# A spectral filter block: the gated spectrum is laid out channel by channel, and the inverse column transform becomes one 128-column and two 64-column matmuls a channel

## The chip, the cores and the metric

The program runs on one core of a Trainium2 chip. The metric is the device time of one execution in microseconds (us); lower is better. Three runs of the kernel before gave 4968.33, 4972.34 and 4972.80 us, median 4972.34 us.

## What is computed

The reference has two layers in a row. The change touches the first one, on x of shape (4 images, 128 rows, 128 columns, 128 channels), all in fp32:

```
f    = fft2(x) over rows and columns, per image and channel
amp  = |f|
gate = sigmoid(amp @ w_h + b_h) + sigmoid(amp @ w_l + b_l)      # a matmul over channels at each frequency
s    = real(ifft2(f * gate))
y    = layernorm(swish(conv3x3(s, w_f) + b_f) + x) * gamma + beta
```

The second layer is a Mamba-like sequence block (projections, a short convolution, a scan over 256 steps in chunks, gating, a feed-forward part). It is not changed, but rows of it are used below.

## The kernel before, in words

The first layer is `spectral_block`. Each engine has a program of its own; they are kept in step by semaphores alone, and each engine runs its instructions in the order written. One image is done after the other (loop `b`, 4 passes). Because x is real, only 65 of the 128 row frequencies are kept; real and imaginary part of the 64 full ones fill 128 rows, and the two edge frequencies (0 and 64), which have one real row each after the first transform, share the slots of row 0.

The stages of an image, with the lines by which the profile names them:

1. **Row transform.** 128 matmuls (L235) of the image's columns against a DFT table. ScalarE (L332) and VectorE (L444) take turns to copy the results from PSUM into `rowspec` [128, 128 frequencies, 128 channels]. The copy goes through PSUM in order and writes each next element 128 words (512 bytes) further on.
2. **Column transform.** Matmuls L250 to L253 by cosine and sine tables; ScalarE and VectorE store the real part, the imaginary part and the amplitude in `spec` [128, 3 x 64, 128 channels]. Before the change its three blocks of 64 rows stand in the order amplitude, real, imaginary.
3. **Gating.** 17 groups (16 of four frequencies, one for the edges) run through a pipeline: TensorE turns the amplitudes (L274), VectorE copies them (L473), TensorE multiplies by the two gate weights (L286), ScalarE takes two sigmoids (L356), VectorE adds them (L480), TensorE turns the sum back (L295), and VectorE multiplies real and imaginary rows by it in place (two instructions of L489 a group; `gate` is read from PSUM). The edges are finished at L496 and L499. In VectorE's program step q does the copy of group q, then the add of group q-1, then the two multiplications of group q-2. GpSimd follows behind each group and writes the negated imaginary rows over the amplitude rows that are no longer needed (L528), so that `spec` holds (-imaginary, real, imaginary).
4. **Inverse column transform.** For each of the 128 channels two matmuls of 128 stationary columns and 128 moving columns accumulate in one PSUM region: L306 has (real, imaginary) of the channel as the stationary operand and the cosine table as the moving one, L307 has (-imaginary, real) and the sine table. The stationary operand of a channel is 128 words that stand 512 bytes apart in `spec`. Both wait for `gated` and for GpSimd's `neg_done`. Every four channels fill one of four PSUM banks; ScalarE (L361) and VectorE (L503) take turns to copy a bank into `rowspec`, now [128, column, channel].
5. **Inverse row transform and 3x3 convolution.** L194 reads `rowspec` column by column, L370 and L398 split the result into two halves in a ring (`s_hi`, `s_lo`), and 27 matmuls for each block of four columns (L211 to L213) make the convolution. Swish, residual and layernorm follow, behind TensorE, and SyncE loads the residual (`xres`) and stores the result. `s_hi`, `s_lo` and the other buffers of this stage lie over `spec`.

In the second layer there are matmuls with 32 stationary columns. `mix` first does two matmuls with 128 stationary columns (L931) and then eight with 32 (L935), one for each head, whose outputs lie on different 32-partition quarters of PSUM:

```
for h in range(HEADS):
    j, low = h // 4, HEADDIM * (h % 4)
    mm = pe.matmul(ps[low:low + HEADDIM, bank, at + j * P:at + (j + 1) * P], dtx[...], mmat[...], ...)
```

An fp32 matmul of the program shows in the trace as two LDWEIGHTS and two MATMUL records, one after the other; so L306 and L307, with 512 matmuls each, have 1024 records each. "Record" below is such a half.

Of the kernel before, what the change touches and what calls it, by code (L numbers as in the profile page):

```python
# [18 lines left out]
ALU = mybir.AluOpType  # L19
ACT = mybir.ActivationFunctionType  # L20

P = 128
IMAGES, H, W, C = 4, 128, 128, 128
# [4 lines left out]
HALF = H // 2  # L28
# [27 lines left out]
def spectral_block(nc, a, z1):  # L56
    ctx = ExitStack()
    counted = []
    with ctx:
# [4 lines left out]
        def sems(name, n):  # L64
# [5 lines left out]

        spec = sb("spec", [P, 3 * HALF, C])

        rowspec = sb("rowspec", [P, P, C])
# [14 lines left out]

        over = Place(nc, "f_", spec_at)
        s_hi = over("s_hi", [P, RING + 2, H + 2], FR)  # L90
        s_lo = over("s_lo", [P, RING + 2, H + 2], FR)
        conv_v = over("conv_v", [P, 2, 512])
        xres = over("xres", [P, 2, 512])
# [13 lines left out]
            sem("f_" + n) for n in ("edge_mm", "edge_copied", "edge_sq", "edge_ss", "edge_amp_ready"))  # L107
        ampT_mm, ampT_ready, gate_mm, sig_ready, gsum_ready, gT_mm, gated, neg_done, edge_scaled = (
            sem("f_" + n) for n in ("ampT_mm", "ampT_ready", "gate_mm", "sig_ready", "gsum_ready",
                                    "gT_mm", "gated", "neg_done", "edge_scaled"))  # L110
        t_mm, t_free = sem("f_t_mm"), sems("f_t_free", 4)
# [76 lines left out]
        def _(pe):  # L188
            def columns(b, j):

                if j >= 4:
                    pe.wait_ge(lo_ready, b * BLOCKS + (j - 3))
                for k in range(4):
                    mm = pe.matmul(ps[:, j % 4, k * P:(k + 1) * P], rowspec[:, 4 * j + k, :], idft_h[:, :],  # L194
                                   start=True, stop=True)
                mm.then_inc(s_mm, 1)
# [31 lines left out]
            with pe.Fori(0, IMAGES) as b:  # L228
# [37 lines left out]
                for q in range(G17 + 2):  # L266
                    if q < G17:
                        if q >= 2:
                            pe.wait_ge(ampT_ready, b * G17 + (q - 1))
                        if q == GROUPS:  # L270
                            pe.wait_ge(edge_amp_ready, b + 1)
                        for k in range(4 if q < GROUPS else 2):
                            src = spec[:, 4 * q + k, :] if q < GROUPS else edge_amp[:, k, :]
                            mm = pe.transpose(ps[:, q % 2, k * P:(k + 1) * P], src, ident[:, :])  # L274
                        mm.then_inc(ampT_mm, 1)
# [23 lines left out]
                pe.wait_ge(gated, b * G17 + G17)  # L299
                pe.wait_ge(neg_done, b * G17 + G17)  # L300
                for j in range(C // 4):
                    if j >= 4:
                        pe.wait_ge(t_free[j % 4], b * 8 + j // 4)
                    for k in range(4):
                        out = ps[:, j % 4, k * P:(k + 1) * P]
                        pe.matmul(out, spec[:, HALF:3 * HALF, 4 * j + k], cosm[:, :], start=True, stop=False)  # L306
                        mm = pe.matmul(out, spec[:, 0:2 * HALF, 4 * j + k], sinm[:, :], start=False, stop=True)  # L307
                    mm.then_inc(t_mm, 1)
# [13 lines left out]
        def _(act):  # L322
# [5 lines left out]
            with act.Fori(0, IMAGES) as b:  # L328
# [6 lines left out]
                with act.Fori(0, GROUPS // 2) as q:  # L335
                    for s in range(2):
                        act.wait_ge(f_mm[s], b * 8 + q + 1)
                        act.activation(spec[:, ds(q * 8 + s * 4 + HALF, 4), :],
                                       ps[:, 2 * s, :].rearrange("p (r c) -> p r c", r=4), ACT.Copy)
                        act.activation(work[:, 2 * s, :], ps[:, 2 * s, :], ACT.Square).then_inc(re_ready[s], 1)  # L340
                        act.wait_ge(ss_ready[s], b * 8 + q + 1)
                        act.activation(spec[:, ds(q * 8 + s * 4, 4), :],
                                       work[:, 4 + s, :].rearrange("p (r c) -> p r c", r=4),
                                       ACT.Sqrt).then_inc(amp_ready[s], 1)
# [14 lines left out]
                for j in range(0, C // 4, 2):  # L359
                    act.wait_ge(t_mm, b * 32 + (j + 1))  # L360
                    act.activation(rowspec[:, :, 4 * j:4 * j + 4],  # L361
                                   ps[:, j % 4, :].rearrange("p (c w) -> p w c", c=4), ACT.Copy).then_inc(t_free[j % 4], 1)
# [23 lines left out]
        def _(dve):  # L386
# [53 lines left out]
            with dve.Fori(0, IMAGES) as b:  # L440
# [8 lines left out]
                with dve.Fori(0, GROUPS // 2) as q:  # L449
                    for s in range(2):  # L450
                        dve.wait_ge(f_mm[s], b * 8 + q + 1)
                        im = spec[:, ds(q * 8 + s * 4 + 2 * HALF, 4), :]
                        dve.tensor_copy(im, ps[:, 2 * s + 1, :].rearrange("p (r c) -> p r c", r=4)).then_inc(im_ready[s], 1)
# [13 lines left out]
                for q in range(G17 + 2):  # L467
# [14 lines left out]
                    if q >= 2:  # L482
                        g = q - 2
                        dve.wait_ge(gT_mm, b * G17 + (g + 1))
                        gate = ps[:, 6 + g % 2, :].rearrange("p (r c) -> p r c", r=4)
                        if g < GROUPS:
                            for row in (HALF + 4 * g, 2 * HALF + 4 * g):
                                part = spec[:, row:row + 4, :]
                                ins = dve.tensor_tensor(part, part, gate, ALU.mult)  # L489
                            ins.then_inc(gated, 1)  # L490
                        else:


                            for k in range(2):
                                part = edge[:, 2 * k:2 * k + 2, :]
                                ins = dve.tensor_tensor(part, part, gate[:, k:k + 1, :].to_broadcast([P, 2, C]), ALU.mult)  # L496
                            ins.then_inc(edge_scaled, 1)
                            dve.wait_ge(edge_scaled, b + 1)
                            dve.tensor_tensor(spec[:, HALF:3 * HALF:HALF, :], edge[:, 0:2, :], edge[:, 2:4, :],  # L499
                                              ALU.add).then_inc(gated, 1)  # L500
                for j in range(1, C // 4, 2):
                    dve.wait_ge(t_mm, b * 32 + (j + 1))
                    dve.tensor_copy(rowspec[:, :, 4 * j:4 * j + 4],  # L503
                                    ps[:, j % 4, :].rearrange("p (c w) -> p w c", c=4)).then_inc(t_free[j % 4], 1)
# [895 lines left out]
```

## Time and profile before

| | |
|---|---|
| median of three runs | 4972.34 us |
| profiled execution | 4973.1 us, span 4971.3 us |
| TensorE matmul busy | 4777.4 us (96%) |
| VectorE busy | 3626.1 us (73%) |
| ScalarE busy | 3136.8 us (63%) |
| GpSimd busy | 1884.9 us (38%) |
| mean granted TensorE clock | 0.983 of full speed |

The span runs from the first to the last instruction of the program; the execution adds 1.8 us around it. A row of the timeline gives the start, the length, engine, line and tiles of a run of like instructions and their count; the length of a merged row is from the first start to the last end. PE is a matmul, PEld a weight load, which may lie beside matmuls. The records of TensorE overlap, since a matmul's record goes on after the next has begun; a busy TensorE is therefore not one at its peak, and the distance of two starts tells more than a duration. PEclk is the granted clock in tenths or as a share of full speed.

### The profile page before, as it was taken

What the parts mean: (1) busy time and instruction counts of PE and PEld (TensorE: products, weight loads), DVE (VectorE), ACT (ScalarE), POOL (GpSimd) and SP (SyncE); (2) the same over time, 40 slices, a digit from 0 to 9 for tenths busy, and PEclk for the clock granted to TensorE, in tenths of its full rate; (3) what the DMA queues carried; (4) which work ended last, traced back from release to release, by engine and by line L of the source; (5) the groups of instructions that cost most, each with busy time, mean ns of one, the idle gap of its engine ahead of it and who ended that gap; (6) DMA issues with size and microseconds to landing.
All of it is one profiled execution on the core that took longest, in us unless ns stands there. A gap on an engine that the chain in (4) does not pass through costs nothing.

```text
span 4971.3 us, 93964 instructions
## 1 busy us (share of the span) xinstructions
PE 4777.4 (96%) x31687; PEld 3555.1 (72%) x31687; DVE 3626.1 (73%) x9341; ACT 3136.8 (63%) x4388; POOL 1884.9 (38%) x2150
## 2 busy tenths in 40 slices
PE   7999999999999999969999999999999999999998
PEld 4888669875988498736766666666667666666766
DVE  4346542655166615659999999999999999999997
ACT  4211421133112411159999999999999999999997
POOL 0011000110011001135566556656655665566564
PEclk9999999999999999979999999999999999999999
DMA  2012201230023001211111111111111111111110
GB/s 78 1 50 70 85 1 35 70 100 0 20 70 99 17 5 62 68 38 37 36 36 36 36 38 36 36 36 36 36 36 38 36 36 36 36 38 36 36 36 24
DMA packets 216359, 205.38 MB, mean 41 GB/s; under 512 B 15904, under 2 KB 150688, under 8 KB 216224
## 3 DMA queue, kind: packets, MB, share of 16 engines
q1 hardware_dynamic: 216224, 203.58, 13.1%
q8 instruction: 85, 1.39, 0.1%
q14 instruction: 50, 0.41, 0.0%
HBM read 136.41 MB, written 67.11 MB: 41 GB/s over the span
## 4 chain that ended last, share of the span: by engine, by line
PE 30%; ACT 23%; issue 3%; DVE 0%; ACTq 0%; POOL 0%; POOLq 0%; DVEq 0%
PE g_ps L935 6%; PE g_ps L931 5%; PE g_ps L874 4%; ACT g_acc L1041 3%; ACT L1101 3%; ACT L1135 3%; PE g_ps L919 3%; ACT g_tap L1046 3%; PE g_ps L903 3%; ACT g_emat L1078 2%; PE g_ps L920 2%; PE g_ps L965 2%; ACT L1098 2%; ACT g_gl L1093 2%; ACT g_bmat L1054 2%
## 5 line engine op out<-in xcount | busy, mean ns | idle before, releaser
L1186 DVE SCALAR_TENSOR_TENSOR g_acc<-g_ps,g_conv_w,g_acc 128x504 f32<-128x504 f32 (+2 forms) x896 | 651.6, 727 | 11.6 <-ACT g_tap L1046 11.6
L1243 DVE TENSOR_TENSOR g_mmat<-g_emat,g_ps 128x1024 f32<-128x1024 f32 x512 | 616.5, 1204 | 1.5 <-PE g_ps L892 0.8
L381 ACT ACTIVATE f_conv_v<-f_ps,f_bias 128x512 f32<-128x512 f32 x128 | 87.9, 687 | 782.3 <-PE f_ps L213 782.3
L1078 ACT ACTIVATE g_emat<-g_ps 128x1024 f32<-128x1024 f32 x512 | 494.4, 1017 | 44.3 <-PE g_ps L920 44.3
L919 PE MATMUL g_ps<-g_rz,g_l 128*128 128x512 f32 x1024 | 481.6, 532 | 27.7 <-ACT g_emat L1078 25.1
L211 PE MATMUL f_ps<-f_s_hi,f_wf_hi 128*128 128x512 f32 x1152 | 468.4, 407 | 2.3 <-DVE f_s_lo L398 2.3
L213 PE MATMUL f_ps<-f_s_hi,f_wf_lo 128*128 128x512 f32 x1152 | 457.9, 397 | 0.0
L212 PE MATMUL f_ps<-f_s_lo,f_wf_hi 128*128 128x512 f32 x1152 | 457.1, 397 | 0.0
L768 POOL TENSOR_TENSOR g_sqs<-g_sq 128x256 f32<-128x256 f32 x256 | 186.7, 729 | 660.6 <-ACT g_sq L1083 660.6
L920 PE MATMUL g_ps<-g_mask_b,g_ident_b 128*128 128x512 bf16 x1024 | 400.2, 391 | 0.0
L540 POOL TENSOR_SCALAR f_rstd<-f_mv 128x4 f32<-128x4 f32 x128 | 40.9, 320 | 839.4 <-DVE f_mv L414 839.4
L503 DVE COPY f_rowspec<-f_ps 128x512 f32<-128x512 f32 x64 | 44.2, 691 | 412.2 <-PE f_ps L307 412.2
L931 PEld LDWEIGHTS g_ps<-g_xs,g_diag 128*128 128x128 f32 x2048 | 277.7, 190 | 88.5 <-issue 88.3
L935 PE MATMUL g_ps<-g_mmat,g_dtx 128*32 128x128 f32 x8192 | 329.8, 279 | 0.0
L773 POOL TENSOR_TENSOR g_acc<-g_acc,g_tap 128x508 f32<-128x508 f32 x256 | 326.1, 1274 | 4.3 <-DVE g_acc L1186 4.3
L931 PE MATMUL g_ps<-g_xs,g_diag 128*128 128x128 f32 x2048 | 326.0, 282 | 1.2 <-ACT g_emat L1078 1.2
L306 PE MATMUL f_ps<-f_cosm,f_spec 128*128 128x128 f32 x1024 | 309.7, 385 | 9.8 <-POOL f_spec L528 9.8
L1284 DVE TENSOR_SCALAR g_hn<-g_z,g_mv,g_r 128x128 f32<-128x128 f32 x512 | 315.9, 676 | 1.7 <-POOL g_r L791 1.7
L307 PE MATMUL f_ps<-f_sinm,f_spec 128*128 128x128 f32 x1024 | 309.3, 384 | 0.0
L361 ACT ACTIVATE f_rowspec<-f_ps 128x512 f32<-128x512 f32 x64 | 38.2, 597 | 417.6 <-PE f_ps L307 417.6
L1041 ACT ACTIVATE g_acc<-g_ps,g_conv_b,g_conv_w 128x512 f32<-128x512 f32 x384 | 283.0, 772 | 6.2 <-PE g_ps L862 6.2
L306 PEld LDWEIGHTS f_ps<-f_cosm,f_spec 128*128 128x128 f32 x1024 | 272.5, 313 | 10.7 <-DVE f_spec L499 10.7
(178 smaller groups left out, 12118.7 us busy)
## 6 DMA issues: line engine op xcount, KB each, us to landing
f_xt<-in_x_cols SPq DMA_DIRECT2D x128, 256.0 KB, 2.9
f_xres<-in_x SPq DMA_DIRECT2D x128, 256.0 KB, 2.7
z<-f_zout SPq DMA_DIRECT2D x128, 256.0 KB, 2.1
g_zin<-z SPq DMA_DIRECT2D x128, 256.0 KB, 2.7
g_zres<-z SPq DMA_DIRECT2D x128, 256.0 KB, 2.7
out<-g_outb SPq DMA_DIRECT2D x128, 256.0 KB, 2.0
f_wf_raw<-in_w_f SPq DMA_DIRECT2D x1, 576.0 KB, 5.1
g_wx<-in_in_proj_t SPq DMA_DIRECT2D x1, 192.0 KB, 2.5
```

The lines of the kernel that those rows point to most:

```text
L211: pe.matmul(out, wf_hi[:, tap, :], hi, start=(tap == 0), stop=False)
L212: pe.matmul(out, wf_hi[:, tap, :], lo, start=False, stop=False)
L213: mm = pe.matmul(out, wf_lo[:, tap, :], hi, start=False, stop=(tap == 8))
L306: pe.matmul(out, spec[:, HALF:3 * HALF, 4 * j + k], cosm[:, :], start=True, stop=False)
L919: pe.matmul(dst, l4[:, g, :], rz[:, 4 * half:4 * half + 4, :], start=True, stop=False)
L920: mm = pe.matmul(dst, ident_b[:, :], mask_b[:, :].unsqueeze(1).to_broadcast([P, 4, P]), start=False, stop=True)
L931: pe.matmul(ps[:, bank, at + j * P:at + (j + 1) * P], diag[:, j, :], xs[:, x.s, j, g, :], start=(g % 2 == 0 and j == 0), stop=False)
L935: mm = pe.matmul(ps[low:low + HEADDIM, bank, at + j * P:at + (j + 1) * P], dtx[:, g // 2, at + HEADDIM * h:at + HEADDIM * (h + 1)], mmat[: ...
L1041: act.activation(acc[:, j], four(ps[:, X_BANK[j] if j < 2 else BC_BANK, :]), ACT.Identity, bias=conv_b[:, j:j + 1], scale=conv_w[:, j, 3:4 ...
L1078: act.activation(emat[:, g, :].rearrange("p (b n) -> p b n", b=2), ps[:, D_BANK[g]:D_BANK[g] + 2, :], ACT.Exp).then_inc(e_a[g], 1)
L1186: dve.scalar_tensor_tensor(out=acc[:, j, :, k:], in0=four(ps[:, bank, :])[:, :, 0:P - k], scalar=conv_w[:, j, 3 - k:4 - k], in1=acc[:, j, ...
L1243: dve.tensor_tensor(mmat[:, g, :].rearrange("p (h n) -> p h n", h=HEADS), emat[:, g, :].rearrange("p (h n) -> p h n", h=HEADS), ps[:, CB, ...
```

## The change

Spectrum: `spec` now has its blocks in the order real, imaginary, amplitude (the indices at stage 2 and in the transposes of stage 3 follow). The gated spectrum is no longer written in place. L489 writes into a new tensor `gains` [128, channel, 128 rows], so that the 128 words of a channel stand side by side; the multiplication's output walks 512 bytes from one element to the next, its inputs are read as before. L499 writes its two rows there too. GpSimd's negation and the semaphore `neg_done` are gone.

Inverse column transform: three matmuls a channel in place of two. The first has all 128 columns of `gains[:, c, :]` as the stationary operand and the cosine table. The second has the 64 imaginary columns and the negated sine table, and writes PSUM partitions 0 to 63. The third has the 64 real columns and the sine table, and writes partitions 64 to 127. Both accumulate onto the first.

Places: `gains` takes the place of `rowspec`; the result of the inverse column transform is a tensor `inv` that takes the place of the real and imaginary rows of `spec`; `s_hi` and `s_lo` lie over `gains`, the other buffers of stage 5 over the amplitude rows. The copies L361 and L503 have the same shapes and strides as before.

```diff
-                pe.wait_ge(neg_done, b * G17 + G17)
                 for j in range(C // 4):
                     if j >= 4:
                         pe.wait_ge(t_free[j % 4], b * 8 + j // 4)
                     for k in range(4):
-                        out = ps[:, j % 4, k * P:(k + 1) * P]
-                        pe.matmul(out, spec[:, HALF:3 * HALF, 4 * j + k], cosm[:, :], start=True, stop=False)
-                        mm = pe.matmul(out, spec[:, 0:2 * HALF, 4 * j + k], sinm[:, :], start=False, stop=True)
+                        at, c = slice(k * P, (k + 1) * P), 4 * j + k
+                        pe.matmul(ps[:, j % 4, at], gains[:, c, :], cosm[:, :], start=True, stop=False)
+                        pe.matmul(ps[0:HALF, j % 4, at], gains[:, c, HALF:], nsinm[:, :], start=False, stop=True)
+                        mm = pe.matmul(ps[HALF:P, j % 4, at], gains[:, c, 0:HALF], sinm[:, :], start=False, stop=True)
                     mm.then_inc(t_mm, 1)
...
-                            for row in (HALF + 4 * g, 2 * HALF + 4 * g):
-                                part = spec[:, row:row + 4, :]
-                                ins = dve.tensor_tensor(part, part, gate, ALU.mult)
+                            for k in range(2):
+                                ins = dve.tensor_tensor(gains[:, :, HALF * k + 4 * g:HALF * k + 4 * g + 4].rearrange("p c r -> p r c"),
+                                                        spec[:, HALF * k + 4 * g:HALF * k + 4 * g + 4, :], gate, ALU.mult)
                             ins.then_inc(gated, 1)
...
-                            dve.tensor_tensor(spec[:, HALF:3 * HALF:HALF, :], edge[:, 0:2, :], edge[:, 2:4, :],
+                            dve.tensor_tensor(gains[:, :, 0:2 * HALF:HALF].rearrange("p c k -> p k c"), edge[:, 0:2, :], edge[:, 2:4, :],
                                               ALU.add).then_inc(gated, 1)
...
-                for g in range(G17):
-                    pool.wait_ge(gated, b * G17 + (g + 1))
-                    pool.sem_inc(waited)
-                    first, last = (max(4 * g, 1), 4 * g + 4) if g < GROUPS else (0, 1)
-                    pool.tensor_scalar(spec[:, first:last, :], spec[:, 2 * HALF + first:2 * HALF + last, :], -1.0, 1.0,
-                                       ALU.mult, ALU.mult).then_inc(neg_done, 1)
```

## Rows read from the trace of the kernel before

**Rows 1.** The page, busy time of each engine (share of the span), instructions

```profile
PE 4777.4 (96%) x31687; PEld 3555.1 (72%) x31687; DVE 3626.1 (73%) x9341; ACT 3136.8 (63%) x4388; POOL 1884.9 (38%) x2150
```

**Rows 2.** Busy time by stretch: gating, inverse column transform, convolution of image 1

```profile
core 0: us, PE busy (x) PEld busy (x) DVE busy (x) ACT busy (x) POOL busy (x), PEclk, DMA share, GB/s
116.00:171.90 55.90, 48.70 (x200) 28.38 (x200) 42.70 (x71) 23.14 (x37) 10.10 (x17) 0.93 0.00 1
171.90:285.50 113.60, 112.76 (x512) 112.60 (x512) 11.06 (x16) 9.55 (x16) 0.62 (x4) 0.98 0.00 1
285.50:532.00 246.50, 245.80 (x1244) 204.78 (x1244) 147.35 (x548) 43.14 (x71) 41.02 (x63) 1.00 0.23 71
```

**Rows 3.** Waits from 172 to 285 us: total, times, longest (us)

```profile
ACT f_rowspec L361 <- PE f_ps L307: 104.5, 16, 8.1
```

**Rows 4.** Timeline, TensorE in the inverse column transform: start, length, count

```profile
178.17 0.60 PE L306 MATMUL f_ps<-f_cosm,f_spec 128*128 128x128 f32 x2
178.61 0.60 PE L307 MATMUL f_ps<-f_sinm,f_spec 128*128 128x128 f32 x2
179.05 0.60 PE L306 MATMUL f_ps<-f_cosm,f_spec 128*128 128x128 f32 x2
```

**Rows 5.** Groups by line, weight loads: busy us, mean ns, idle before

```profile
L306 PEld LDWEIGHTS f_ps<-f_cosm,f_spec 128*128 128x128 f32 x1024 | 272.5, 313 | 10.7 <-DVE f_spec L499 10.7
L194 PEld LDWEIGHTS f_ps<-f_idft_h,f_rowspec 128*128 128x128 f32 x1024 | 135.6, 195 | 14.8 <-issue 4.2
```

**Rows 6.** Timeline, 128-column and 32-column matmuls in turn (second layer), then their loads

```profile
2514.06 0.61 PE L931 MATMUL g_ps<-g_xs,g_diag 128*128 128x128 f32 x4
2514.60 0.65 PE L935 MATMUL g_ps<-g_mmat,g_dtx 128*32 128x128 f32 x16
2515.17 0.71 PE L931 MATMUL g_ps<-g_xs,g_diag 128*128 128x128 f32 x4
2515.81 0.64 PE L935 MATMUL g_ps<-g_mmat,g_dtx 128*32 128x128 f32 x16
...
2514.60 0.38 PEld L935 LDWEIGHTS g_ps<-g_mmat,g_dtx 128*32 128x32 f32 x16
2515.17 0.52 PEld L931 LDWEIGHTS g_ps<-g_xs,g_diag 128*128 128x128 f32 x4 [0.20 <-issue]
```

**Rows 7.** One line's durations (min/median/max ns), and a run of 128-column matmuls

```profile
L935 PE MATMUL g_ps<-g_mmat,g_dtx x8192: 272/273/298, 2190.2 to 4947.9; 128*32 128x128 f32 x200
...
2504.35 1.95 PE L953 MATMUL g_ps<-g_wc,g_ygt 128*128 128x128 f32 x16
```

**Rows 8.** Timeline, VectorE in the gating stage, one round of two groups

```profile
151.02 0.68 DVE L473 COPY f_work<-f_ps 128x512 f32<-128x512 f32 x1
153.61 0.68 DVE L473 COPY f_work<-f_ps 128x512 f32<-128x512 f32 x1
155.07 0.69 DVE L480 TENSOR_TENSOR f_work<-f_work 128x512 f32<-128x512 f32 x1 [0.78 <-ACT f_work L356]
155.68 1.28 DVE L489 TENSOR_TENSOR f_spec<-f_spec,f_ps 128x512 f32<-128x512 f32 x2
156.88 0.68 DVE L473 COPY f_work<-f_ps 128x512 f32<-128x512 f32 x1
```

**Rows 9.** Groups by line, VectorE: busy us, mean ns, idle before

```profile
L489 DVE TENSOR_TENSOR f_spec<-f_spec,f_ps 128x512 f32<-128x512 f32 x128 | 81.7, 680 | 0.0
L503 DVE COPY f_rowspec<-f_ps 128x512 f32<-128x512 f32 x64 | 44.2, 691 | 412.2 <-PE f_ps L307 412.2
L444 DVE COPY f_rowspec<-f_ps 128x512 f32 x64 | 65.8, 1036 | 85.2 <-PE f_ps L235 77.7 <-issue 7.5
```

**Rows 10.** Timeline, the last steps of the gating stage

```profile
170.91 0.42 DVE L499 TENSOR_TENSOR f_spec<-f_edge 128x256 f32<-128x256 f32 x1
171.52 0.30 POOL L528 TENSOR_SCALAR f_spec<-f_spec 128x128 f32<-128x128 f32 x1 [0.50 <-DVE f_spec L499]
171.97 0.78 PE L306 MATMUL f_ps<-f_cosm,f_spec 128*128 128x128 f32 x2 [2.46 <-POOL f_spec L528]
```

**Rows 11.** Busy time by stretch, the first 4.1 us of the transform (granted clock: 0.50)

```profile
172.00:176.10 4.10, 4.10 (x19) 4.10 (x20) 0.00 (x0) 0.24 (x1) 0.00 (x0) 0.50 0.00 0
```

More of the change, by code:

```diff
@@ L71, in spectral_block @@
         spec = sb("spec", [P, 3 * HALF, C])
+        row_at = sb.at
         rowspec = sb("rowspec", [P, P, C])
@@ L87, in spectral_block @@
         mhalf = sb("mhalf", [P, 4])
-        over = Place(nc, "f_", spec_at)
+        amp_at = row_at - HALF * C * 4
+        gains = Place(nc, "f_", row_at)("gains", [P, C, 2 * HALF])
+        inv = Place(nc, "f_", spec_at)("inv", [P, W, C])
+        over = Place(nc, "f_", row_at)
         s_hi = over("s_hi", [P, RING + 2, H + 2], FR)
         s_lo = over("s_lo", [P, RING + 2, H + 2], FR)
+        over = Place(nc, "f_", amp_at)
         conv_v = over("conv_v", [P, 2, 512])
@@ L107, in spectral_block @@
             sem("f_" + n) for n in ("edge_mm", "edge_copied", "edge_sq", "edge_ss", "edge_amp_ready"))
-        ampT_mm, ampT_ready, gate_mm, sig_ready, gsum_ready, gT_mm, gated, neg_done, edge_scaled = (
+        ampT_mm, ampT_ready, gate_mm, sig_ready, gsum_ready, gT_mm, gated, edge_scaled = (
             sem("f_" + n) for n in ("ampT_mm", "ampT_ready", "gate_mm", "sig_ready", "gsum_ready",
-                                    "gT_mm", "gated", "neg_done", "edge_scaled"))
+                                    "gT_mm", "gated", "edge_scaled"))
         t_mm, t_free = sem("f_t_mm"), sems("f_t_free", 4)
@@ L193, in columns @@
                 for k in range(4):
-                    mm = pe.matmul(ps[:, j % 4, k * P:(k + 1) * P], rowspec[:, 4 * j + k, :], idft_h[:, :],
+                    mm = pe.matmul(ps[:, j % 4, k * P:(k + 1) * P], inv[:, 4 * j + k, :], idft_h[:, :],
                                    start=True, stop=True)
@@ L272, in _ @@
                         for k in range(4 if q < GROUPS else 2):
-                            src = spec[:, 4 * q + k, :] if q < GROUPS else edge_amp[:, k, :]
+                            src = spec[:, 2 * HALF + 4 * q + k, :] if q < GROUPS else edge_amp[:, k, :]
                             mm = pe.transpose(ps[:, q % 2, k * P:(k + 1) * P], src, ident[:, :])
@@ L337, in _ @@
                         act.wait_ge(f_mm[s], b * 8 + q + 1)
-                        act.activation(spec[:, ds(q * 8 + s * 4 + HALF, 4), :],
+                        act.activation(spec[:, ds(q * 8 + s * 4, 4), :],
                                        ps[:, 2 * s, :].rearrange("p (r c) -> p r c", r=4), ACT.Copy)
@@ L341, in _ @@
                         act.wait_ge(ss_ready[s], b * 8 + q + 1)
-                        act.activation(spec[:, ds(q * 8 + s * 4, 4), :],
+                        act.activation(spec[:, ds(q * 8 + s * 4 + 2 * HALF, 4), :],
                                        work[:, 4 + s, :].rearrange("p (r c) -> p r c", r=4),
@@ L360, in _ @@
                     act.wait_ge(t_mm, b * 32 + (j + 1))
-                    act.activation(rowspec[:, :, 4 * j:4 * j + 4],
+                    act.activation(inv[:, :, 4 * j:4 * j + 4],
                                    ps[:, j % 4, :].rearrange("p (c w) -> p w c", c=4), ACT.Copy).then_inc(t_free[j % 4], 1)
@@ L451, in _ @@
                         dve.wait_ge(f_mm[s], b * 8 + q + 1)
-                        im = spec[:, ds(q * 8 + s * 4 + 2 * HALF, 4), :]
+                        im = spec[:, ds(q * 8 + s * 4 + HALF, 4), :]
                         dve.tensor_copy(im, ps[:, 2 * s + 1, :].rearrange("p (r c) -> p r c", r=4)).then_inc(im_ready[s], 1)
@@ L502, in _ @@
                     dve.wait_ge(t_mm, b * 32 + (j + 1))
-                    dve.tensor_copy(rowspec[:, :, 4 * j:4 * j + 4],
+                    dve.tensor_copy(inv[:, :, 4 * j:4 * j + 4],
                                     ps[:, j % 4, :].rearrange("p (c w) -> p w c", c=4)).then_inc(t_free[j % 4], 1)
```

## The prediction, written before the result was known

> **What bounds the kernel now.** I read the page's busy times first. TensorE is busy for 96% of the span and no other engine for more than 73% [rows 1], but that is an average over two layers, and the change touches two stages of one. So the next view is the busy time by stretch. In image 1 the gating stage takes 55.9 us and the inverse column transform 113.6 us; the other three images show the same lengths within 1 us. In the transform VectorE and ScalarE work for 11 and 10 us of it, and matmuls and weight loads both fill it [rows 2]. The waits of that stretch agree: ScalarE's copies wait 104.5 us for L307 [rows 3]. What TensorE needs for a channel is what the stage costs, with nothing behind it to take over: the four copies of 16 columns go on at 3.5 us a bank, and one takes 0.7 us.
>
> The timeline gives the price of a channel. L306 starts at 178.17, L307 at 178.61, the next L306 at 179.05: 0.44 us a matmul, 0.88 a channel, and 128 of them make 112.6 of the 113.6 us [rows 4]. That is 0.22 a record. Elsewhere TensorE is twice as fast with the same shape: 16 records of L953 in 1.95 us, the last of which takes 0.27, are 1.68 / 15 = 0.112 a record [rows 7]. The weight loads show why: one of L306, whose words stand 512 bytes apart, takes 313 ns, one of L194, whose words stand side by side, 195 [rows 5]. The transform is bound by strided weight loads.
>
> The gating stage has another bound. VectorE is busy for 42.7 of 55.9 us and TensorE for 48.7 [rows 2], but neither is full; it is a ring of dependences. The copy of a group starts at 151.02, and the add of the same group at 155.07, when its sigmoid is there: 4.05 us, in which another group's copy (153.61) is slipped in and VectorE idles for 0.78. From 155.07 to the copy at 156.88 are the add and two multiplications. So two groups take 4.05 + 1.81 = 5.86 us, and only every second group's multiplications lie on that ring [rows 8].
>
> **The transform after the change.** All its weight loads become contiguous, so a record costs 0.112 and not 0.22. Two matmuls of 128 columns would then take 0.45 us a channel. But there are three matmuls, and TensorE has to change between 128-column and 64-column form twice a channel, 1024 times in all. The second layer shows what such a change costs, with 32 columns for 64 [rows 6]. The last record of L931 starts at 2514.06 + 0.61 - 0.27 = 2514.40, and the first load of L935 only at 2514.60, 0.20 later, where a load otherwise lies beside the matmul before it. The last record of L935 starts at 2514.98, and the next load of L931 at 2515.17, again 0.20 later, after an idle time of 0.20 that the row itself shows; its first product then has to wait for that load too. The whole turn of 4 records with 128 columns and 16 with 32 takes 2515.81 - 2514.60 = 1.21 us. The 16 lie beside each other: their starts span 0.65 - 0.27 = 0.38 us, which is four rounds of four (three steps of 0.112, 0.025 for the first load, since the longest of its records takes 298 ns and the median 273 [rows 7], 0.02 of issue). So each quarter of the columns has its own queue, and neighbours in program order that use one quarter don't hold up the others.
>
> A channel has 2 records with 128 columns and 4 with 64, on two halves: two rounds. Against the 1.21 us that is two full records less (0.224), two rounds less (0.224), and a first load of 64 columns in place of 32 (0.025 more): 1.21 - 0.224 - 0.224 + 0.025 = 0.79 us. It saves 0.88 - 0.79 = 0.09 us a channel, for 512 channels 46 us. Bounds: with no cost of the changes of form, four rounds, 0.45 us (220 us saved); with the four records of the sine part one after the other, 0.79 + 0.22 = 1.01 us (67 us lost). I take 0.79, since rows 6 are the nearest thing to the new loop.
>
> The Trainium skill has a rule that would put the price higher. TensorE: Matmul & The Clock Gate, "The mechanism" in its part on packing small matmuls, says that matmuls are strictly first in, first out in start and end. Each sine matmul is two records on one half of the columns, so by that rule the order would be first half, then both halves at once, then second half: three rounds for two. Rows 6 speak against it: in the same order the 16 records of L935 would need nine rounds, and their starts would span 8 x 0.112 = 0.9 us where they span 0.38.
>
> **The clock.** At the start of the transform the granted clock is 0.50 for 4.1 us, and costs nothing today, since the weight loads set the pace [rows 11]: 19 records in 4.1 us are 0.22 each, as later [rows 4]. The matmuls on TensorE just before are sparse (the last groups of the gating), and that stays. After the change a round takes 0.21 us at 1.2 GHz and not 0.11, a channel 0.79 + 4 x 0.107 = 1.22. In 4.1 us 3.4 channels are done and not 5.2: 1.4 us an image, 6 in all. Bounds 0 and, if the slow stretch were twice as long, 12.
>
> **The gating after the change.** L489 now walks 512 bytes from one written element to the next. L444 writes in just this way, from PSUM, with the same shape: 1036 ns, where L503, which writes 16 bytes at a stride, takes 691 and L489 today 680 [rows 9]. So a multiplication grows by 0.355 us. Bounds: 0.01 (as L503) and 0.5. On the ring of rows 8 one group's two multiplications lie, so two groups take 5.86 + 0.71 = 6.57 us; VectorE's own work for two groups (four multiplications at a distance of 0.95, two copies and two adds at 0.60) is 6.2, still below. Seven times 0.71, and the last two groups, behind which nothing waits any more, with 0.71 each: 6.4 us an image. If instead every group's growth counted, 16 x 0.71 = 11.4.
>
> The end of the stage gets shorter. L499 starts at 170.91, GpSimd's last negation at 171.52, the first matmul at 171.97 [rows 10]. The negation's 0.30 and the hop to it go, 0.6 us less; L499 writes 256 elements at the stride and grows by half of 0.355, 0.2 more. The other 16 negations were behind VectorE and cost nothing. Sum of the gating: 6.4 - 0.6 + 0.2 = 6.0 us an image, 24 us in all; from -2 to +44 by the bounds.
>
> **At no cost.** The copies L361 and L503 keep their shape, and a bank comes every 3.2 us and not 3.5. The order of `spec` changes places and no strides. `wf_raw`, `xres` and `zout` lie elsewhere; SyncE's loads start on the same counts, and the next image's first copies write over `s_hi` and `s_lo` only behind matmuls that TensorE issues after its last convolution, so they wait for nothing new. L194 reads `inv` as it read `rowspec`. With the gating slower, ScalarE and TensorE idle more in it; both have room.
>
> **The sum.** -46 + 6 + 24 = -16 us against the profiled execution's 4973.1 us, 4957.1; that execution was 0.8 us above the median of the three runs, so 4956 us. Only 0.03 us a channel lies between this and no gain: it breaks even at 0.82 us.
>
> **Rivals.**
> - The sine matmuls take three rounds, because their two records on one half follow each other. The place is the transform, the price 0.112 x 512 = 57 us: 5013 us, slower. It decides as soon as a channel costs over 0.82 us. For it speaks that no row has 64-column matmuls, against it rows 6. With four rounds, 5070.
> - The strided multiplication costs nothing, as L503's stride does: -46 + 6 - 2 = -42, 4930 us. Against it, L444 has the same stride and L503 has not.
> - VectorE becomes the bound in the gating: the ring breaks up and each group pays 0.71. 16 x 0.71 - 0.4 = 11 us an image, 44 in all: +4, 4976 us, no change. For it speaks that 6.57 and 6.2 are close.
> - The changes of form cost less with 64 columns, as low as the step of 0.112 between rounds. A channel takes some 0.6 us, 143 us saved: about 4860 us. Against it, both directions show 0.20.
> - The clock stays at 1.2 GHz through the transform, since TensorE now pauses 1024 times. A channel takes 1.22: (1.22 - 0.88) x 512 + 24 = 198, 5170 us. Against it, the turns of rows 6 run at full speed, in a stage with denser work around them.
>
> **How the numbers follow.** The forecast has 0.50, with a range of its own of 4940 to 4975. Three rounds 0.15, four 0.04, a free stride 0.10, VectorE as the bound 0.12, cheap changes of form 0.05, the slow clock 0.04. A measurement of this kernel can tell 0.2% (10 us) from no change. Below 4962 lie some 0.36 of the forecast's 0.50, the free stride and the cheap changes: 0.51 faster. The rest of the forecast and VectorE's case, 0.26, are no change. Three and four rounds and the clock, 0.23, are slower. The range goes from 4915 to 5015 us: it holds the forecast, the free stride, VectorE's case and three rounds, and leaves out 0.13 and a little of the edges.
>
> **What would show it.** In the trace after, the distance of two cosine matmuls should be 0.79 us (0.60, 0.90 or 1.22 for the rivals), the weight loads of 128 columns some 190 ns and not 313, and an idle time of 0.20 before each of them. The transform should take 102 to 103 us an image and not 113.6, the gating 62 and not 55.9. L489 should take 1.04 us, with two groups every 6.6 us. The prediction is wrong if a channel costs over 0.82 us or under 0.75, or if the gating grows by over 10 us or not at all.

## The result: 263 us slower, and the transform ran at half clock

The changed kernel takes 5233.08 us (median of 4 runs, 5231.5 to 5236.5) against 4970.35 us for the kernel before in the same comparison: a ratio of 1.0529, 95% interval 1.0511 to 1.0548. The forecast was 4956 us, in a range of 4915 to 5015, so the sign and the size are both wrong. The span of the profiled execution is 5234.7 us and the mean granted clock 0.918 where it was 0.983.

The page after, busy time of each engine and the line of the granted clock in 40 slices (9 is 90% or more of full speed):

```profile
PE 5030.0 (96%) x32711; PEld 3521.4 (67%) x32711; DVE 3660.9 (70%) x9341; ACT 3136.0 (60%) x4388; POOL 1840.7 (35%) x2082
PEclk9669995899669995897999999999999999999999
```

TensorE is 96% busy as before [rows 1]; the busy share says nothing of the loss. The clock line does: it dips once in each of the four images (the single 7 behind them stands in the line of the kernel before too). The same three stretches of image 1 as in [rows 2] show where:

```profile
core 0: us, PE busy (x) PEld busy (x) DVE busy (x) ACT busy (x) POOL busy (x), PEclk, DMA share, GB/s
117.70:177.60 59.90, 49.09 (x200) 27.50 (x201) 51.09 (x71) 22.94 (x37) 0.00 (x0) 0.97 0.00 1
177.60:351.50 173.90, 173.01 (x769) 102.12 (x769) 11.07 (x16) 9.55 (x16) 0.53 (x4) 0.50 0.00 1
351.50:600.00 248.50, 247.79 (x1244) 206.67 (x1244) 147.61 (x549) 43.50 (x71) 40.25 (x62) 0.99 0.22 71
```

The inverse column transform takes 173.9 us and not 113.6, with a granted clock of 0.50 throughout. In the four images it is 173.9, 174.2, 173.9 and 174.2 us, 242 us more in all. The gating takes 59.9, 58.2, 59.8 and 58.2 us, 15 more in all. The remaining 6 of 263 us lie outside these two stages, where no stretch grew by more than 2.5 us. A part of them is the start of the stage behind the transform, where the clock is still down for 4.0 us in image 1 before it comes back:

```profile
351.50:355.50 4.00, 4.00 (x19) 4.00 (x20) 0.69 (x1) 0.83 (x2) 0.00 (x0) 0.50 0.81 243
```

The timeline of TensorE after, its start, then a later channel and the start of the next, then the weight loads of that channel; it answers to [rows 4]:

```profile
177.60 0.49 PE L311 MATMUL f_ps<-f_cosm,f_gains 128*128 128x128 f32 x2 [2.56 <-DVE f_gains L505]
...
178.64 0.80 PE L311 MATMUL f_ps<-f_cosm,f_gains 128*128 128x128 f32 x2
...
200.30 0.80 PE L311 MATMUL f_ps<-f_cosm,f_gains 128*128 128x128 f32 x2
201.03 0.48 PE L312 MATMUL f_ps<-f_nsinm,f_gains 128*64 128x128 f32 x1
201.03 0.48 PE L313 MATMUL f_ps<-f_sinm,f_gains 128*64 128x128 f32 x1
201.29 0.42 PE L312 MATMUL f_ps<-f_nsinm,f_gains 128*64 128x128 f32 x1
201.30 0.42 PE L313 MATMUL f_ps<-f_sinm,f_gains 128*64 128x128 f32 x1
201.65 0.80 PE L311 MATMUL f_ps<-f_cosm,f_gains 128*128 128x128 f32 x2
```

```profile
200.30 0.50 PEld L311 LDWEIGHTS f_ps<-f_cosm,f_gains 128*128 128x128 f32 x2 [0.33 <-issue]
201.02 0.18 PEld L312 LDWEIGHTS f_ps<-f_nsinm,f_gains 128*64 128x64 f32 x1 [0.23 <-issue]
201.03 0.18 PEld L313 LDWEIGHTS f_ps<-f_sinm,f_gains 128*64 128x64 f32 x1
201.08 0.23 PEld L312 LDWEIGHTS f_ps<-f_nsinm,f_gains 128*64 128x64 f32 x1
201.09 0.23 PEld L313 LDWEIGHTS f_ps<-f_sinm,f_gains 128*64 128x64 f32 x1
```

A channel takes 201.65 - 200.30 = 1.35 us. L312 and L313 lie beside each other and their four records are two rounds, as the forecast had it. The first cosine pair, at 177.60, still has the length of 2.4 GHz (0.49 us for two); the next, at 178.64, has 0.80. In image 1 the clock falls within the first microsecond of the stage. Before the change it was down at the same place, at 0.50 from the first matmul at 171.97 to 177.1, which is 5.2 us and not only the 4.1 us that [rows 11] cover (in image 2 it was 3.4 us). Now it doesn't come back before the stage is over. The stretch in the kernel before at which [rows 11] break off:

```profile
176.10:177.10 1.00, 1.00 (x6) 1.00 (x6) 0.00 (x0) 0.36 (x1) 0.00 (x0) 0.50 0.00 0
```

### The profile page after: what moved, and what is told of

It reads as the page before. It is cut to its first block, busy times and chain, and to the rows that moved or that the text cites. A ratio compares the mean times of both kernels' runs of the same rounds, so it can differ in the third digit from the quotient of the medians.

```text
span 5234.7 us, 95907 instructions
## 1 busy us (share of the span) xinstructions
PE 5030.0 (96%) x32711; PEld 3521.4 (67%) x32711; DVE 3660.9 (70%) x9341; ACT 3136.0 (60%) x4388; POOL 1840.7 (35%) x2082
## 4 chain that ended last, share of the span: by engine, by line
PE 28%; ACT 22%; issue 3%; DVE 0%; ACTq 0%; POOL 0%; POOLq 0%; DVEq 0%
PE g_ps L934 6%; PE g_ps L930 5%; PE g_ps L873 4%; ACT g_acc L1040 3%; ACT L1100 3%; ACT L1134 3%; PE g_ps L918 3%; ACT g_tap L1045 3%; PE g_ps L902 3%; ACT g_emat L1077 2%; PE g_ps L919 2%; PE g_ps L964 2%; ACT L1097 2%; ACT g_gl L1092 2%; ACT g_bmat L1053 2%
## 5 line engine op out<-in xcount | busy, mean ns | idle before, releaser
L509 DVE COPY f_inv<-f_ps 128x512 f32<-128x512 f32 x64 | 44.3, 692 | 651.5 <-PE f_ps L313 651.5
L367 ACT ACTIVATE f_inv<-f_ps 128x512 f32<-128x512 f32 x64 | 38.2, 597 | 653.0 <-PE f_ps L313 653.0
L311 PE MATMUL f_ps<-f_cosm,f_gains 128*128 128x128 f32 x1024 | 407.6, 501 | 10.2 <-DVE f_gains L505 10.2
L311 PEld LDWEIGHTS f_ps<-f_cosm,f_gains 128*128 128x128 f32 x1024 | 257.1, 313 | 178.6 <-issue 167.4
L313 PE MATMUL f_ps<-f_sinm,f_gains 128*64 128x128 f32 x1024 | 352.9, 448 | 0.0
L312 PE MATMUL f_ps<-f_nsinm,f_gains 128*64 128x128 f32 x1024 | 352.9, 448 | 0.0
```

Source lines behind the costliest of these rows:

```text
L311: pe.matmul(ps[:, j % 4, at], gains[:, c, :], cosm[:, :], start=True, stop=False)
L312: pe.matmul(ps[0:HALF, j % 4, at], gains[:, c, HALF:], nsinm[:, :], start=False, stop=True)
```

## The experiments

Theory A: the pauses at the changes of form keep the clock down. Its rival B: records of 64 columns do. Theory C: the stream only fails to regain a clock once lost, and would hold it. Its rival D: it cannot hold it. Beyond that, the gating's price is taken apart, and better forms are tried. All times "before" stand for the kernel before, run on the same chip in the same comparison.

### e1: no change of form within the stage

```diff
-                        pe.matmul(ps[:, j % 4, at], gains[:, c, :], cosm[:, :], start=True, stop=False)
+                        pe.matmul(ps[0:HALF, j % 4, at], gains[:, c, 0:HALF], cosm[:, :], start=True, stop=False)
+                        pe.matmul(ps[HALF:P, j % 4, at], gains[:, c, HALF:], cosm[:, :], start=True, stop=False)
```

> The changed kernel with the cosine matmul split in two as well: every matmul of the inverse column transform has 64 stationary columns, four a channel, so TensorE never changes form inside the stage. The result is the same. Theory A (the two changes of form a channel leave TensorE idle, and that keeps the clock at 1.2 GHz once it has fallen): no idle time, clock 1.00 but for the first few us, eight records on two halves are four rounds of 0.112, 0.45 us a channel, the transform 58 us an image and not 172, about 5233 - 4 x 114 = 4777 us. Theory B (matmuls and loads of 64 columns count too little for the clock, whatever stands between them): the clock stays at 0.50, four rounds of 0.213 and slower loads, 0.9 to 1.2 us a channel, 5000 to 5150 us.

Measured: 4764.04 us, ratio to before 0.9581 (0.9565 to 0.9597). A second and a third comparison gave 4765.96 us (0.9585, 0.9569 to 0.9601) and 4768.60 us (0.9594, 0.9581 to 0.9607). The transform took 58.7, 59.3, 58.6 and 58.5 us. The start of the transform (its first matmul is at 176.88) and the rest of it, then a channel and the start of the next:

```profile
176.90:180.90 4.00, 4.00 (x44) 4.00 (x46) 0.00 (x0) 0.47 (x1) 0.00 (x0) 0.57 0.01 4
182.00:236.00 54.00, 53.12 (x970) 52.90 (x967) 11.06 (x16) 8.96 (x15) 0.53 (x4) 1.00 0.01 2
```

```profile
200.00 0.27 PE L311 MATMUL f_ps<-f_cosm,f_gains 128*64 128x128 f32 x1
200.00 0.27 PE L312 MATMUL f_ps<-f_cosm,f_gains 128*64 128x128 f32 x1
200.10 0.27 PE L311 MATMUL f_ps<-f_cosm,f_gains 128*64 128x128 f32 x1
200.11 0.27 PE L312 MATMUL f_ps<-f_cosm,f_gains 128*64 128x128 f32 x1
200.21 0.27 PE L313 MATMUL f_ps<-f_nsinm,f_gains 128*64 128x128 f32 x1
...
200.43 0.27 PE L311 MATMUL f_ps<-f_cosm,f_gains 128*64 128x128 f32 x1
```

One channel is 0.43 us in four rounds of two records. The clock is down for most of the first 4 us (0.57) and then at 1.00 to the end of the stage. Theory B is wrong: the stage has nothing but 64-column records here. One more matmul a channel, and 469 us less than the changed kernel.

### e2: the changes of form once a bank

```diff
-                        pe.matmul(ps[:, j % 4, at], gains[:, c, :], cosm[:, :], start=True, stop=False)
-                        pe.matmul(ps[0:HALF, j % 4, at], gains[:, c, HALF:], nsinm[:, :], start=False, stop=True)
-                        mm = pe.matmul(ps[HALF:P, j % 4, at], gains[:, c, 0:HALF], sinm[:, :], start=False, stop=True)
+                        pe.matmul(ps[:, j % 4, at], gains[:, c, :], cosm[:, :], start=(k == 0), stop=False)
+                    for k in range(4):
+                        at, c = slice(k * P, (k + 1) * P), 4 * j + k
+                        pe.matmul(ps[0:HALF, j % 4, at], gains[:, c, HALF:], nsinm[:, :], start=False, stop=(k == 3))
+                        mm = pe.matmul(ps[HALF:P, j % 4, at], gains[:, c, 0:HALF], sinm[:, :], start=False, stop=(k == 3))
```

> The changed kernel with the matmuls of a bank (four channels) reordered: first the four cosine matmuls of 128 columns, then the eight sine matmuls of 64. The result is the same, the changes of form are a quarter. Theory A: TensorE is at work for most of the time again, the clock comes back to 1.00, 8 records with 128 columns and 16 with 64 (8 rounds) are 1.8 us plus two changes of 0.2 and a first load, 2.3 us a bank, 0.57 a channel, the transform 74 us an image, about 4840 us. Theory B: the clock stays at 0.50, over 1.0 us a channel, above 5050 us.

Measured: 4815.98 us, ratio 0.9687 (0.9671 to 0.9703). The transform took 70.1, 71.3, 70.7 and 70.0 us, 0.55 a channel. The first 4 us of the transform and a stretch within it:

```profile
177.60:181.60 4.00, 3.80 (x25) 3.24 (x26) 0.15 (x1) 0.00 (x1) 0.00 (x0) 0.57 0.00 0
184.00:247.00 63.00, 63.00 (x719) 54.21 (x718) 10.09 (x15) 8.96 (x15) 0.00 (x0) 1.00 0.01 1
```

The same records as the changed kernel in another order: a quarter of the changes of form, and the clock comes back after the same start.

### e3: dense work ahead of the transform

```diff
                 pe.wait_ge(gated, b * G17 + G17)
+                for _n in range(16):
+                    pe.matmul(ps[:, 3, :], ident[:, :], xt[:, 0, :], start=True, stop=True)
```

> The changed kernel with 16 dense matmuls of 512 columns ahead of each transform, whose result is not used (some 14 to 17 us an image of added work), so that TensorE enters the stage at 2.4 GHz. Theory C (the clock is only not regained: the stream holds it once it has it): the transform at 0.79 us a channel, 101 us an image, in all about 5233 - 4 x 71 + 65 = 5015 us. Theory D (the stream cannot hold it either): the clock falls again within the stage and the channel is back at 1.35 us, about 5290 us.

Measured, in one run: 5006.03 us, where the runs of before in that comparison have a median of 4972.19. So with 63 us of added, useless work (15.5 in image 1, from 177.90 to 193.44) it is 227 us faster than the changed kernel. Each transform took 101.7 us. A stretch around the dense matmuls, the stretch at 0.50 within them, and the transform behind them; then one channel of the stream, which is not altered:

```profile
174.00:192.00 18.00, 14.54 (x31) 6.39 (x32) 3.81 (x7) 0.00 (x0) 0.00 (x0) 0.91 0.00 0
178.20:181.60 3.40, 3.40 (x5) 1.33 (x4) 0.00 (x0) 0.00 (x0) 0.00 (x0) 0.50 0.00 0
193.00:293.00 100.00, 100.00 (x762) 62.78 (x760) 10.36 (x15) 9.55 (x16) 0.00 (x0) 1.00 0.00 1
```

```profile
194.91 0.49 PE L313 MATMUL f_ps<-f_cosm,f_gains 128*128 128x128 f32 x2
195.32 0.32 PE L314 MATMUL f_ps<-f_nsinm,f_gains 128*64 128x128 f32 x1
...
195.69 0.49 PE L313 MATMUL f_ps<-f_cosm,f_gains 128*128 128x128 f32 x2
196.11 0.32 PE L314 MATMUL f_ps<-f_nsinm,f_gains 128*64 128x128 f32 x1
196.12 0.32 PE L315 MATMUL f_ps<-f_sinm,f_gains 128*64 128x128 f32 x1
```

195.69 - 194.91 = 0.78; over the stage it is 101.7 less the tail of about 1, by 128, 0.79 us: the price that the prediction had taken from the second layer. The clock falls here too, 0.3 us into the dense work, so what stands before the transform makes it fall, and not the changed stream; the dense work brings it back. With the clock at 1.00 on entry, the stream holds it for 100 us, in all four images. Theory D falls.

### e5: the same dense work in the middle of the transform

```diff
+                    if j == 16:
+                        for _n in range(16):
+                            pe.matmul(ps[:, 4, :], ident[:, :], gains[:, 0:4, :], start=True, stop=True)
```

> The changed kernel with 16 dense matmuls of 512 columns put in the middle of each transform, after channel 64 of 128; their result is not used (some 14 to 20 us an image of added work). Theory C (the clock falls in the sparse end of the gating and this stream holds whichever clock it enters with): the first 64 channels at 1.35 us each, 87 us, the other 64 at 0.79, 50 us; about 5233 - 4 x 36 + 65 = 5155 us. Theory E (in the run with the dense matmuls ahead of the transform the clock held for some reason tied to the start of the stage): both halves at 1.35, about 5300 us.

Measured, in one run: 5148.57 us (before in that comparison: 4972.72). The first 64 channels, the dense matmuls (264.39 to 279.68) with the stream's first channels behind them, and the rest of the second 64:

```profile
178.00:264.00 86.00, 85.88 (x382) 50.84 (x384) 4.90 (x8) 4.78 (x8) 0.00 (x0) 0.50 0.00 1
264.00:282.00 18.00, 18.00 (x55) 8.31 (x53) 0.69 (x1) 0.00 (x0) 0.00 (x0) 0.91 0.00 1
284.00:331.00 47.00, 46.12 (x354) 28.94 (x353) 5.54 (x8) 4.18 (x7) 0.53 (x4) 1.00 0.00 1
```

One and the same stream runs for 86 us at 0.50 and then, after dense work, at 1.00 to its end. The clock that it enters with decides. Theory C holds in both places, and E falls.

### e6: the changes of form once in two channels

```diff
...
+                    for k2 in range(0, 4, 2):
+                        for k in (k2, k2 + 1):
+                            at, c = slice(k * P, (k + 1) * P), 4 * j + k
+                            pe.matmul(ps[:, j % 4, at], gains[:, c, :], cosm[:, :], start=(k == k2), stop=False)
+                        for k in (k2, k2 + 1):
+                            at, c = slice(k * P, (k + 1) * P), 4 * j + k
+                            pe.matmul(ps[0:HALF, j % 4, at], gains[:, c, HALF:], nsinm[:, :], start=False, stop=(k == k2 + 1))
+                            mm = pe.matmul(ps[HALF:P, j % 4, at], gains[:, c, 0:HALF], sinm[:, :], start=False, stop=(k == k2 + 1))
```

> The changed kernel with the matmuls reordered by two channels: two cosine matmuls of 128 columns, then four sine matmuls of 64; half the changes of form, the same result. At 2.4 GHz it is 0.787 us for one channel plus two records and two rounds of 0.112 more for the second, 1.23 us a pair, 0.62 a channel, 79 us an image; at 1.2 GHz 1.35 + 4 x 0.213 = 2.2 a pair, 141 us an image. Theory A (the clock comes back once the pauses are a small enough share): 79 us and about 4855 us if a share of about a third is small enough, otherwise 141 us and about 5100 us.

Measured: 4857.35 us, ratio 0.9771 (0.9754 to 0.9787). The transform took 82.2, 81.1, 82.2 and 81.7 us, 0.63 a channel. The start (its first matmul is at 173.99) and the rest of it:

```profile
174.00:179.80 5.80, 5.80 (x30) 4.47 (x32) 0.00 (x0) 0.60 (x1) 0.00 (x0) 0.50 0.00 0
182.00:255.00 73.00, 73.00 (x716) 55.66 (x717) 9.97 (x15) 8.96 (x15) 0.00 (x0) 1.00 0.00 1
```

Half of the changes of form are few enough: the clock is down for the first 5.8 us and then at 1.00. Nothing between this kernel and the changed one was run. The reordering by pairs gives 376 us against the changed kernel.

### e4: the gating's strided write

```diff
-                                ins = dve.tensor_tensor(gains[:, :, HALF * k + 4 * g:HALF * k + 4 * g + 4].rearrange("p c r -> p r c"),
+                                ins = dve.tensor_tensor(gains[:, HALF * k + 4 * g:HALF * k + 4 * g + 4, :],
```

> The changed kernel with the gating's products written side by side as before the change and not at a stride of 512 bytes; this leaves the layout of the gated spectrum out. The transform is left as it is. It prices the strided write: L494 should take 0.68 us and not 1.04. By the prediction's ring the gating loses 6 us an image, 24 in all: about 5209 us. If VectorE's growth is partly hidden, as the trace after suggests (the stage grew by 3 to 5 us an image), 12 to 18: about 5218 us. If every group paid, 44: 5189 us.

This kernel leaves out the channel-by-channel layout: the products are written row by row, while the transform still reads them channel by channel. So it does not compute the filter, and serves only to price the write.

Measured: 5213.66 us, ratio to before 1.0486 (1.0468 to 1.0503), 19.4 us less than the changed kernel had in its comparison, or 21 less if each is taken against its own kernel before. The gating took 54.8, 54.6, 54.5 and 56.1 us, 16 less in all. L494 in the changed kernel and, below, in this one:

```profile
L494 DVE TENSOR_TENSOR f_gains<-f_spec,f_ps 128x512 f32<-128x512 f32 x128 | 123.0, 1040 | 0.0
```

```profile
L494 DVE TENSOR_TENSOR f_gains<-f_spec,f_ps 128x512 f32<-128x512 f32 x32 | 20.5, 681 | 0.0
```

The duration of the strided write is the predicted one to a few ns, 1040 for 1036, and its effect a little less than the 24 us of the ring.

### e7: 64 columns throughout, with strided loads

```diff
-        gains = Place(nc, "f_", row_at)("gains", [P, C, 2 * HALF])
+        gains = Place(nc, "f_", row_at)("gains", [P, 2 * HALF, C])
...
+                        pe.matmul(ps[0:HALF, j % 4, at], gains[:, 0:HALF, c], cosm[:, :], start=True, stop=False)
+                        pe.matmul(ps[HALF:P, j % 4, at], gains[:, HALF:2 * HALF, c], cosm[:, :], start=True, stop=False)
...
-                                ins = dve.tensor_tensor(gains[:, :, HALF * k + 4 * g:HALF * k + 4 * g + 4].rearrange("p c r -> p r c"),
+                                ins = dve.tensor_tensor(gains[:, HALF * k + 4 * g:HALF * k + 4 * g + 4, :],
...
```

> All matmuls of the inverse column transform with 64 stationary columns, as in e1_halves, but the gated spectrum stays in rows as before the change: the gating writes side by side, the weight loads are strided by 512 bytes. The result is the same. Theory F (the loads of the two halves of the columns run beside each other, so that a strided load of 64 words takes half of the time of one of 128 and stays hidden behind the 0.112 of a round): the transform 59 to 62 us, the gating back at 55 us, about 4764 - 17 = 4747 us. Theory G (a strided word costs the same wherever it goes, one after the other): 4 x 64 words twice a channel as before the change with 2 x 128 twice, 0.88 us a channel, 113 us an image, about 4965 us.

Measured: 4823.81 us, ratio 0.9700 (0.9684 to 0.9717); e8, the kernel of e1 on the same chip, 4765.96. The transform took 77.9, 78.3, 78.5 and 77.8 us, 0.60 a channel; the gating 53.0 to 56.0. One line's loads and matmuls:

```profile
L311 PE MATMUL f_ps<-f_cosm,f_gains 128*64 128x128 f32 x246 | 56.5, 312 | 0.0
L311 PEld LDWEIGHTS f_ps<-f_cosm,f_gains 128*64 128x64 f32 x245 | 49.2, 254 | 0.0
```

Neither theory: a round takes 0.60 / 4 = 0.15 us, between F's 0.11 and G's 0.22. The whole kernel is 149 us faster than the kernel before, with the gated spectrum row by row as there. 142 of them lie in the transform, whose loads walk the same words at the same stride, in halves. The others come with the separate tensor and without GpSimd's negation. Beside e1, which has the same matmuls, it prices the stride of the loads: 0.15 us a round against 0.11. What limits a strided round at 0.15 was not found.

> The kernel of e1_halves once more, on this chip beside e7_strided_halves, so that the two can be compared: 4764 us, the same within 0.2%.

### e9: the gating's product in pieces of 16 bytes

```diff
-                                ins = dve.tensor_tensor(gains[:, :, HALF * k + 4 * g:HALF * k + 4 * g + 4].rearrange("p c r -> p r c"),
-                                                        spec[:, HALF * k + 4 * g:HALF * k + 4 * g + 4, :], gate, ALU.mult)
+                                ins = dve.tensor_tensor(gains[:, :, HALF * k + 4 * g:HALF * k + 4 * g + 4],
+                                                        spec[:, HALF * k + 4 * g:HALF * k + 4 * g + 4, :].rearrange("p r c -> p c r"),
+                                                        gate.rearrange("p r c -> p c r"), ALU.mult)
```

> e1_halves with the gating's multiplication walked in another order: channel by channel, four rows each, so that it writes pieces of 16 bytes and reads its two inputs (spectrum in SBUF, gate in PSUM) with a stride of 512 bytes. The result is the same. Theory H (only a write of single words at a stride is slow; L509, which reads PSUM at a stride and writes pieces of 16 bytes, takes 692 ns): the multiplication 0.69 us, the gating back at 55 us and not 60, about 4765 - 18 = 4747 us. Theory I (a strided read in SBUF costs what the strided write costs): 1.04 us and 4765 us, no change.

Measured: 4777.95 us, ratio 0.9614 (0.9601 to 0.9627), and e10, e1's kernel beside it, 4768.60 us (0.9594, 0.9581 to 0.9607). So it is no gain, and 9 us slower by the medians, with no run of the one within the range of the other. The multiplication, then the two multiplications of one group here and in e10:

```profile
L495 DVE TENSOR_TENSOR f_gains<-f_spec,f_ps 128x512 f32<-128x512 f32 x32 | 32.0, 1041 | 0.0
...
153.37 2.01 DVE L495 TENSOR_TENSOR f_gains<-f_spec,f_ps 128x512 f32<-128x512 f32 x2
```

```profile
152.78 1.93 DVE L495 TENSOR_TENSOR f_gains<-f_spec,f_ps 128x512 f32<-128x512 f32 x2
```

1041 ns again: with a strided read in SBUF the multiplication takes what it takes with the strided write (theory I). Both inputs are strided here, but L509, which reads PSUM at the same stride, takes only 692 ns in the changed kernel, so the SBUF input is the one that costs. The stride can be moved from the output to the input, not away. The gating took 61.2 to 61.3 us in each image here, against 58.2 to 59.9 in e10. The two multiplications of a group take 0.07 to 0.08 us longer together, for 16 groups about 1.2 us an image; why, and where the rest goes, is not shown.

> The kernel of e1_halves beside e9_pieces on one chip, to compare the two: 4765 us.

## Why the prediction was wrong, step by step

**The stage's bound, and why: right.** TensorE alone set the transform's length, and the loads of strided words were the reason for 0.22 us a record: with the same 64-column matmuls a round takes 0.15 us with strided loads (e7) and 0.11 with contiguous ones (e1).

**The price of a channel, 0.79 us: right at full clock, not what happened.** e3 shows 0.79 with the changed stream. The three parts were right too: two rounds for the sine matmuls, 0.20 us at each change of form, and the queue for each part of the columns. The rival with three rounds did not occur, and the rule of strict order in the Trainium skill (TensorE: Matmul & The Clock Gate, "The mechanism"), which the prediction weighed, is not what this trace shows: L312's second record starts at 201.29, after L313's first at 201.03, though it stands before it in the program.

**The clock: this is the step that failed.** The prediction said that the clock is 0.50 for 4.1 us at the start of each transform, and let it come back after the same time as before. It took the recovery for a matter of time, and priced it at 6 us, 12 at most. (The 4.1 us are the length of the stretch in [rows 11], not of the slow clock, which lasted 5.2 us in that image; this misreading alone would have changed the sum by about a microsecond.) Against the 101.7 us a transform of e3, the half clock costs 72 us an image, some 290 in all, in place of the 6. But the kernel before got its clock back in [rows 11] with a stream that left TensorE no pause: at half clock its loads and rounds still fill it back to back. The changed stream pauses twice a channel, for 0.33 and 0.23 us by its loads' rows, and never gets it back. The same row that gave "4.1 us" shows the dense stream, with loads busy for 4.10 of 4.10 us, and the prediction did not carry it over. In its place the runs show: clock lost within about two microseconds of the transform's start, behind the gating's sparse end, as before, whatever work follows (changed kernel, e1, e2, e3); not regained at a change of form every channel (changed kernel, and for 86 us in e5); regained at a change every two channels (e6), every four (e2) or never (e1); held once dense work has brought it back (e3, e5). That it is the pauses which count, and not something else in a change of form, is the likely reading and not shown: no run had the same pauses without a change of form.

**The rival with the slow clock had the mechanism, with a chance of 0.04 and a size too small.** It said 1.22 us a channel and 5170 us; measured are 1.35 and 5233. The rounds were counted at 0.213, but the pauses and the first loads too get longer, and 0.13 us a channel for 512 channels are 67 us. In the trace after, the load of L311 begins 201.65 - 201.30 = 0.35 us after the last sine record, where it was 0.20 at full clock, and by the groups of the trace after L311's loads, though contiguous, take 313 ns in the mean, where L194's take 195 [rows 5] and the same loads in e3, at full clock, 186 to 190. (That 313 is also the mean of the strided loads before is chance.) The argument against it, that [rows 6] run at full speed among denser work, was no argument against it: rows 6 show that a stream with such pauses runs on at a full clock that it already has, as e3 shows of the changed stream itself. They say nothing of regaining the clock, and the changed stream enters without it.

**The gating: right in kind, 24 us predicted, 15 measured.** (e4's stages give the strided write 16 us, its time 19 to 21.) The write took 1040 ns and the negation's tail went. Two groups of VectorE in image 1 after:

```profile
151.40 0.67 DVE L479 COPY f_work<-f_ps 128x512 f32<-128x512 f32 x1
152.49 0.69 DVE L486 TENSOR_TENSOR f_work<-f_work 128x512 f32<-128x512 f32 x1 [0.42 <-ACT f_work L362]
153.10 1.94 DVE L494 TENSOR_TENSOR f_gains<-f_spec,f_ps 128x512 f32<-128x512 f32 x2
154.88 0.67 DVE L479 COPY f_work<-f_ps 128x512 f32<-128x512 f32 x1
...
157.83 0.69 DVE L479 COPY f_work<-f_ps 128x512 f32<-128x512 f32 x1
```

157.83 - 151.40 = 6.43 us for two groups, against 5.86 in [rows 8] and 6.57 predicted. One group's two multiplications hold VectorE for 154.88 - 153.10 = 1.78 us, where it was 156.88 - 155.68 = 1.20. So two groups grew by 0.57 and one pair by 0.58: the ring still decides, as it was said, and VectorE still idles for 0.42 in it. The term that was too large is the 0.71: the instruction grew by 0.36 us, but the next one starts only 0.29 later.

**The sum.** Predicted: -46 + 6 + 24. Measured: 242 for the transform, 15 for the gating, and 6 elsewhere. At the entry clock of e3 the transform is 12 us an image shorter than before, 48 in all, as forecast (46).

## What to carry to other kernels

A short stretch at low clock in the trace of before has two sides: what made it fall, and what work brought it back. Before replacing the work that stands there, ask whether the new work, at half clock, is as dense as the old. If it is not, it may still bring the clock back, as in e2 and e6, or fail to; price the whole stage at half clock, with its loads and pauses, and give that a fair chance. Do not alternate between one matmul of 128 stationary columns and one pair of 64 where the clock can be lost: group them, or split the wide ones so that all have one form, even for one more matmul. Here that turned a loss of 5.3% into a gain of 4.1 to 4.2% over the kernel before.

## What the runs showed of the hardware that was not expected

- What clock a stream gets can depend on the clock that it enters with. The same instruction stream runs for 86 us at 0.50, and after 15.5 us of dense matmuls for the rest of the stage at 1.00 (e5).
- Two matmuls of 64 stationary columns on the two halves cost the time of one with 128: four take 0.43 us (e1), where one of 128 with contiguous loads takes 2 x 0.112 us [rows 7].
- Splitting a matmul with strided loads in two halves lowers the price of a strided load: 0.15 us a round of two 64-column records (e7) against 0.22 for a record of 128 columns [rows 4].
- VectorE pays for 512-byte steps between single words in an SBUF input as in its output: 1041 and 1040 ns for 512 elements a partition, against 681 side by side (e9, the changed kernel, e4) and 692 with the steps in a PSUM input and pieces of 16 bytes in the output (L509).
